# Two context loads of a period, issued behind the second k moves instead of between q's write and its reads

## The reference

```
qh = softmax(Wq @ layernorm(x), over the 64 rows of a head) * 64**-0.5
kh = softmax(Wk @ ctx, over the 1024 columns)
vh = Wv @ ctx
context = kh @ vh.T                    # per head, 64 x 64
out = Wo @ (context.T @ qh) + bo
x = x + out / |out| * g * sqrt(128)
x = x + gate * feed_forward(layernorm(x))
```

## Time and profile before

| | before |
|---|---|
| median of three runs | 762.15 us |
| profiled execution | 765.37 us, its span 763.6 us |
| mean granted TensorE clock | 0.919 |
| TensorE matmul busy | 642.6 us (84%) |
| VectorE busy | 542.8 us (71%) |
| ScalarE busy | 419.1 us (55%) |
| GpSimd busy | 409.7 us (54%) |
| SyncE's DMA queue, as a share of 16 engines | 48.6% |

### The profile page before, as it was taken

One profiled execution on the slowest core, in us unless ns is written; L12 is line 12 of the kernel. 1 busy time (PEld: TensorE's weight loads), 2 busy tenths in 40 slices (PEclk: granted clock), 3 DMA queues, 4 the chain that ended last, 5 costly groups with the idle time before them and its releaser, 6 DMA issues.

```text
span 763.6 us, 11451 instructions
## 1 busy us (share of the span) xinstructions
PE 642.6 (84%) x3718; PEld 552.2 (72%) x3718; DVE 542.8 (71%) x721; ACT 419.1 (55%) x864; POOL 409.7 (54%) x421
## 2 busy tenths in 40 slices
PE   5877888888888989796969696979796849999896
PEld 4757677777776868685859594859585839999674
DVE  6795959595959586868686777686866462575797
ACT  5444546464646464646555555455545354767584
POOL 5742537374747465656565655565647262542095
PEclk9898979899999999999999999888999889999999
DMA  8855646565656464747474747374627350000046
GB/s 300 169 163 121 191 113 187 120 187 118 194 119 194 113 196 112 201 104 201 106 205 102 206 101 209 88 206 100 181 65 226 62 151 2 1 1 2 1 175 267
DMA packets 63531, 106.12 MB, mean 139 GB/s; under 512 B 11392, under 2 KB 43680, under 8 KB 61168
## 3 DMA queue, kind: packets, MB, share of 16 engines
q1 hardware_dynamic: 62432, 101.62, 48.6%
q0 software_dynamic: 896, 2.45, 1.2%
q10 hardware_dynamic: 144, 1.31, 0.4%
HBM read 46.62 MB, written 25.17 MB: 94 GB/s over the span
## 4 chain that ended last, share of the span: by engine, by line
PE 58%; DMA 26%; DVE 7%; issue 5%; SPq 3%; ACT 1%; POOL 0%; DVEq 0%; ACTq 0%; POOLq 0%
PE ob L560 15%; DMA q_hd<-q_turned 14%; PE gm L530 10%; DMA q_turned<-qt 10%; PE gm L616 4%; PE turn L616 3%; PE k_slot L488 3%; DVE qsum L1236 3%; PE k_slot L489 3%; DVE qt L1249 3%; PE k_slot L490 3%; SPq L424 2%; PE q_slot L488 2%; PE q_slot L490 2%; PE q_slot L489 2%
## 5 line engine op out<-in xcount | busy, mean ns | idle before, releaser
L1050 POOL TENSOR_TENSOR qs_sb<-qs_sb,qrec 128x1024 f32<-128x1024 f32 x64 | 121.8, 1904 | 239.9 <-DVE qrec L1240 239.9
L560 PE MATMUL ob<-mt_sb,q_hd 128*128 128x128 f32 x1024 | 152.8, 312 | 69.5 <-DMA q_hd<-q_turned 69.0
L560 PEld LDWEIGHTS ob<-mt_sb,q_hd 128*128 128x128 f32 x1024 | 144.1, 223 | 82.0 <-DMA q_hd<-q_turned 77.9
L1204 DVE TENSOR_REDUCE nkm<-k_slot 128x1 f32<-128x1024 f32 x62 | 75.2, 1213 | 136.7 <-PE k_slot L490 136.7
L800 ACT ACTIVATE ek<-k_slot,nkm 128x1024 f32<-128x1024 f32 x62 | 69.1, 1115 | 187.0 <-DVE nkm L1204 185.5
L530 PE MATMUL gm<-ekT,ctxT 128*128 128x256 f32 x512 | 133.4, 414 | 28.2 <-issue 28.2
L530 PEld LDWEIGHTS gm<-ekT,ctxT 128*128 128x128 f32 x512 | 104.4, 206 | 50.5 <-issue 33.9
L810 ACT ACTIVATE qs_sb<-qs_sb 128x1024 f32<-128x1024 f32 x64 | 67.8, 1060 | 39.7 <-DVE qs_sb L1229 39.7
L1223 DVE TENSOR_REDUCE qm<-q_slot 128x16 f32<-128x1024 f32 x64 | 76.0, 1188 | 15.9 <-PE q_slot L490 15.6
L1236 DVE TENSOR_REDUCE qsum<-qs_sb 128x16 f32<-128x1024 f32 x64 | 77.4, 1209 | 3.7 <-ACT qs_sb L810 3.7
L1229 DVE TENSOR_TENSOR qs_sb<-q_slot,qm 128x1024 f32<-128x1024 f32 x64 | 78.4, 1225 | 2.2
(11 more groups left out here) (208 smaller groups left out, 1297.6 us busy)
## 6 DMA issues: line engine op xcount, KB each, us to landing
ekT<-kt SPq DMA_DIRECT2D x496, 64.0 KB, 2.1
q_turned<-qt SPq DMA_DIRECT2D x16, 1024.0 KB, 4.8
q_hd<-q_turned SPq DMA_DIRECT2D x64, 256.0 KB, 5.5
ctx_in<-ctx_rows SPq DMA_DIRECT2D x16, 512.0 KB, 6.8
x_all<-x SPq DMA_DIRECT2D x16, 512.0 KB, 3.6
ctxT<-ctx_cols SPq DMA_DIRECT2D x16, 512.0 KB, 5.8
out<-q_hd SPq DMA_DIRECT2D x15, 512.0 KB, 2.7
Wuq_in<-Wuq_cols ACTq DMA_DIRECT2D x1, 1280.0 KB, 6.9
```

Of the source, the lines that this page charges most:

```text
L560: last = nc.tensor.matmul(ob[:, (j % 4) * C:(j % 4 + 1) * C], q, mt_sb[:, b % 2, t, :], start=(t == 0), stop=(t == T - 1))
L1050: nc.gpsimd.tensor_tensor(e, e, qrec[:, i % 2, :].unsqueeze(2).broadcast_to([P, PAIR, DH]), ALU.mult).then_inc(q_mul, 1)
L1204: V.tensor_reduce(nkm[:, i:i + 1], k_psum(b, i)[:, :], AX, ALU.max, negate=True).then_inc(k_max, 1)
```

## The change

SyncE's order within a period is changed, and nothing else. Before, the two loads were issued between `q_out` and `q_in`; now they are issued behind `move_k(b, 1)`. The order of q's write, its reads and the k moves among each other stays. In the last round (b = 16) the tables of the second layer are loaded as before.

```
                 if has(b - 1):
                     q_out(b - 1)
+                if has(b - 1):
+                    q_in(b - 1)
+                if has(b):
+                    move_k(b, 1)
                 if 2 <= b < B:
                     load_ctxT(b)
                 if 2 <= b + 2 < B:
                     load_ctx(b + 2)
-                if has(b - 1):
-                    q_in(b - 1)
-                if has(b):
-                    move_k(b, 1)
-                else:
+                if b == B:
                     ffn_tables()
```

## The result

The changed kernel takes 888.43 us (median of four runs, 886.45 to 890.37), the kernel before 763.14 us in the same comparison. The ratio is 1.164, with a 95% interval from 1.159 to 1.169. The forecast was 887 us.

The account below looks back on a forecast made before the run. It took a loop to bound the kernel, with TensorE's L530 waiting for ctxT without slack; 13 periods at 9.1 us more and a last at 7.1 make 125 us: 887 us, range 860 to 930.

Parts of the forecast that it names:

- ctxT has no slack: TensorE uses ctxT in the period that loads it; L530 starts 0.14 us after its landing, ahead of L560.
- Write to L530: From q's write to TensorE's L530: 3.81 + 1.85 + 10.5 + 3.6 + 0.14 = 19.9 us, against 6.33 today.
- the rival with shared engines: ctxT and ctx_in share the DMA engines, so ctxT lands in 5.8 us: 31 us more, 918 us; chance 0.10.
- The restart: TensorE after idling: L530 at the low clock, L560 mostly at the high one, 5.5 us for both (3.5 to 6.9).
- The rest of the period: From the k product behind L560 to the next write: same instructions, TensorE gapless, so it moves along unchanged.
- the sum: Write to k product 25.4 us against 16.3: 9.1 more in 13 periods, 7.1 in the last, together 125 us.
- The rival that expects part to be given back: The tail from TensorE's last gapless product to the next write halves from 3.85 us: 25 less, 862 us; chance 0.07.
- The first two periods: In periods 0 and 1 only ctx_in moves: counted as 0, between -2 and +4 us.
- The reads decide: If ctxT came in time, earlier and faster reads of q save 1.87 us a period: 736 us or more gain; chance 0.03.

Follow-up runs that it names:

- e1: Kernel before, but only the ctx_in loads go behind the second k moves; ctxT stays between q's write and its reads: 759.54 us, ratio 0.996.
- e2: Kernel before, but only the ctxT loads go behind the second k moves; ctx_in stays between q's write and its reads: 899.69 us, ratio 1.180.
- e3: Changed kernel, but ctxT is issued after 8 of the 16 second k moves, ctx_in still behind all of them: 840.0 us.
- e4: Changed kernel, but ctxT is issued after q's reads, ahead of all second k moves; ctx_in stays behind them: 803.87 us, ratio 1.055.
- e5: Changed kernel, but ctxT is issued ahead of its period's first k moves; ctx_in stays behind the second k moves: 754.67 us, ratio 0.990.
- e6: Kernel before, but ctxT is issued ahead of its period's first k moves; ctx_in stays between q's write and its reads: 758.41 us, ratio 0.997.
- e0: The kernel before, unchanged, run once more for a second profile of its first 50 us: 757.58 us.
- e9: e5, but batch 2's ctx_in load in its old place and the whole first half of G in TensorE's step 0: 736.12 us, ratio 0.966.

## Why the prediction was right

The prediction went mainly by one turn of the trace before, and one turn after is shown above. The table has the means, in us, of the 13 full periods from the second write of q to the 15th; k product stands for the first one behind L560.

| | before | forecast | changed kernel |
|---|---|---|---|
| write to L530 | 6.25 | 19.9 | 19.67 |
| L530 to the k product | | 5.5 | 5.80 |
| write to the k product | 16.11 (taken: 16.3) | 25.4 | 25.47 |
| k product to the next write | 21.80 | unchanged | 21.45 |
| period | 37.91 | 47 | 46.92 |

*ctxT has no slack.* The step that decided was to read the "issue" ahead of L530 as a wait for ctxT, from 0.14 us between landing and start. e1 and e2 show that it is this load, e3 and e4 that its place sets the time; in e5 and e6, where ctxT comes early, the wait is gone.

*Write to L530.* Predicted 19.9 us, measured 19.47 in the turn shown. The write without a load behind it took 3.80 (predicted 3.81), reads and moves 379.33 - 367.23 = 12.10 (12.35), ctxT's landing 3.5 (3.6). The second load behind ctxT did not slow it: the rival with shared engines (918 us) fell. In e1, with no ctx_in behind it, ctxT still lands 5.7 us after its issue; so the 5.8 of before came with the write ahead of it, not with the company. e3 and e4 show what does slow a load, its neighbours in the queue: 3.5 us behind all sixteen moves, 5.3 between two halves of them close behind the reads, 7.4 right behind the reads. The Trainium skill, "DMA: Bandwidth & Descriptors", section "Queues, rings and completion order", says that descriptors of a ring are consumed in order; the landings of the turn shown agree: by their medians ctxT lands at 382.83, ctx_in behind it at 380.02 + 4.2 = 384.22 and x behind that at 380.45 + 5.6 = 386.05.

*The restart.* Predicted 5.5 us, measured 5.80 on the mean, between 4.89 and 6.51; the turn shown (389.41 - 382.90 = 6.51) is the longest. L530 ran at the low level, as predicted (0.50 in this turn). L560 took 1.70 to 2.97 us, 2.32 on the mean, nearer to the high level's 1.7 than to the low level's 3.42, as predicted too; in this turn it ran at 0.55.

*The rest of the period.* This was forecast to move along unchanged, and in the turns shown it does: 410.85 - 389.41 = 21.44, before 350.35 - 328.92 = 21.43. But the prediction had read one of the four periods of the trace before in which the granted clock is 1.00 in the first 1.6 us from the k product. In the other nine it is 0.50 to 0.80; in the first period the k product takes 0.77 us instead of 0.47, and the rest 124.13 - 101.83 = 22.30. In the changed kernel it is 1.00 in all 13 periods. So 0.35 us a period came back (0.2 against the second profile of before, e0), 4.6 us in all, which no term of the sum had. The rival that expects part to be given back (862 us) named another place, the tail behind TensorE's last product, and 25 us; it fell.

A period lost 9.0 us (predicted 9.1), the 14th 7.2 (7.1). That the period is met so closely is in part luck: the time before was taken 0.2 us too long, and 0.35 came back.

*The first two periods.* I counted 0, between -2 and +4. The profiles differ by -3.9, outside these ends; by e0 that is the first profile's own start. One wait is there: ScalarE waits once for batch 2's ctx_in.

```profile
ACT ctx_hi L782 <- DMA ctx_in<-ctx_rows: 3.1, 1, 3.1
```

*The reads decide.* The reads went out earlier, and that bought nothing while ctxT came after them. e5 gives that rival its conditions. It priced them at 26 us or more; they are worth about 8 (0.990). On the mean of 13 periods L560 starts 1.5 us earlier after the write than before (11.36 against 12.86; the rival has 1.87). TensorE's idle time is in one piece and about as long in all, and in the first 1.6 us from the k product the granted clock is 0.50 in nine of the 13 periods, before in two, where the rival had expected the clock to gain.

## What to carry to other kernels

In a queue issued in program order, a load's place sets its arrival: count the issues that it is moved past (here 20, 12 us) and compare with the gap between its landing and its first use, before counting what its absence frees. An idle time labelled "issue" can be a DMA wait: check whether a load of that instruction's operand landed just before its start. A load whose buffer is free long before its use belongs ahead of the period's other transfers, and work that it enables belongs into the wait that is left; here the early load alone gave 0.997 (e6), with q's write freed of loads as well 0.990 (e5), and with that work moved into the wait 0.966 (e9).

## What was not expected of the hardware

A single 512 KB load issued right behind the 1 MB write put off the reads that wait for it by 1.0 us (4.82 against 3.80; ctx_in's load in e2 and e6, ctxT's in e1), and two such loads by hardly more (4.88). So it isn't the bytes behind the write that cost it. What does was not tried.
